# Scores of linear attention in 32x64 tiles of TensorE, without the quarter above the diagonal

## The reference

```python
qp = _phi(proj(Wq, bq)); kp = _phi(proj(Wk, bk)); v = proj(Wv, bv)      # _phi = elu + 1
def step(carry, inp):
    kv, ksum = carry
    kt, vt, qt = inp
    kv = kv + einsum('bhd,bhe->bhde', kt, vt)
    ksum = ksum + kt
    num = einsum('bhd,bhde->bhe', qt, kv)
    den = einsum('bhd,bhd->bh', qt, ksum)[..., None] + EPS
    return ((kv, ksum), num / den)
x = x + _linear_attn(_layernorm(x), ...) @ Wo.T + bo
x = x + ffn(_layernorm(x), gate_w, w1, b1, w2, b2)
```

## Time and profile before

| | us |
|---|---|
| median of 3 runs | 1938.83 (1938.12 to 1944.05) |
| the profiled execution | 1939.27 |
| its span in the profile | 1937.6 |
| PE, DVE, POOL, ACT busy | 1904.0, 1586.2, 891.4, 664.3 |
| mean granted clock of TensorE | 0.997 |

### The profile page before, as it was taken

One profiled execution on the slowest core, in us unless ns is written; L12 is line 12 of the kernel. 1 busy time (PEld: TensorE's weight loads), 2 busy tenths in 40 slices (PEclk: granted clock), 3 DMA queues, 4 the chain that ended last, 5 costly groups with the idle time before them and its releaser, 6 DMA issues. The chain is left out here.

```text
span 1937.6 us, 60626 instructions
## 1 busy us (share of the span) xinstructions
PE 1904.0 (98%) x25412; PEld 1671.4 (86%) x25412; DVE 1586.2 (82%) x3379; ACT 664.3 (34%) x1297; POOL 891.4 (46%) x979
## 2 busy tenths in 40 slices
PE   7999999999999999999999999999999999999997
PEld 6788888888888888888888888888888888888886
DVE  6878878887879888778878987887788897878787
ACT  4333333333333233333333333333332333323331
POOL 4355443455443554534554445545345544355422
PEclk9999999999999999999999999999999999999998
DMA  6343234433343432333423334323433334333222
GB/s 202 94 133 106 92 111 125 127 110 104 100 127 110 128 118 74 127 121 115 122 99 105 116 111 138 113 85 111 132 116 116 98 96 129 113 126 119 75 72 84
DMA packets 171202, 218.03 MB, mean 113 GB/s; under 512 B 24369, under 2 KB 85809, under 8 KB 170929
## 3 DMA queue, kind: packets, MB, share of 16 engines
q1 hardware_dynamic: 168528, 213.59, 34.7%
q10 hardware_dynamic: 2400, 0.55, 0.1%
HBM read 151.02 MB, written 63.04 MB: 110 GB/s over the span
## 5 line engine op out<-in xcount | busy, mean ns | idle before, releaser
L1258 POOL TENSOR_TENSOR k_sum<-k_sum,q_raw 128x512 f32<-128x512 f32 x128 | 165.0, 1290 | 556.2 <-DVE q_raw L933 556.2
L836 ACT ACTIVATE e_tmp<-ring,bias_n 128x512 f32<-128x512 f32 x256 | 176.1, 688 | 509.9 <-PE ring L651 506.8
L922 DVE TENSOR_TENSOR s_mask<-ring,causal 128x512 f32<-128x512 f32 x512 | 314.9, 678 | 0.0
L669 PE MATMUL ring<-wv_hi,xt_hi 128*128 128x260 f32 x1024 | 299.3, 292 | 0.0
L669 PE MATMUL ring<-wo_hi,o_hi 128*128 128x260 f32 x1024 | 287.8, 282 | 1.2 <-ACT o_hi L886 1.0
L669 PE MATMUL ring<-wv_lo,xt_hi 128*128 128x260 f32 x1024 | 288.8, 282 | 0.0
L669 PE MATMUL ring<-wv_hi,xt_lo 128*128 128x260 f32 x1024 | 288.8, 282 | 0.0
L669 PE MATMUL ring<-wo_lo,o_hi 128*128 128x260 f32 x1024 | 288.4, 282 | 0.0
L669 PE MATMUL ring<-wo_hi,o_lo 128*128 128x260 f32 x1024 | 287.3, 284 | 0.9 <-DVE o_lo L1170 0.9
L886 ACT ACTIVATE o_hi<-num_ps 128x512 fp32r<-128x512 f32 x128 | 76.4, 597 | 475.0 <-PE num_ps L750 474.9
L651 PE MATMUL ring<-xt_hi,wk_hi 128*128 128x512 f32 x512 | 207.9, 406 | 5.2 <-DVE xt_lo L998 3.2
(11 more groups left out here) (140 smaller groups left out, 4060.3 us busy)
## 6 DMA issues: line engine op xcount, KB each, us to landing
x_tok<-in_x SPq DMA_DIRECT2D x128, 256.0 KB, 3.7
res<-in_x SPq DMA_DIRECT2D x128, 256.0 KB, 2.8
out<-res SPq DMA_DIRECT2D x128, 256.0 KB, 2.1
x_in<-in_x_t SPq DMA_DIRECT2D x124, 256.0 KB, 4.6
keys_turned<-k_turned SPq DMA_DIRECT2D x112, 256.0 KB, 2.0
k_tok<-keys_turned SPq DMA_DIRECT2D x448, 64.0 KB, 2.0
x_rows<-moments_rows SPq DMA_DIRECT2D x31, 512.0 KB, 3.7
k_t<-in_wk_t SPq DMA_DIRECT2D x4, 256.0 KB, 8.3
```

Source lines behind the costliest of these rows:

```text
L669: mm = pe.matmul(bank[:, 0:HW], rows[a](k), w[b][:, k, h, :], start=n == 0, stop=n == 3 * KD - 1)
L836: act.activation(e_tmp[:, m], bank, ACT.Relu, bias=bias_n[:, m, g:g + 1], scale=-1.0).then_inc(phi_relu.handle, 1)
L922: dve.tensor_tensor(s_mask[:, j], ring[:, st.bank(u)].rearrange("p (g t) -> p g t", g=KD), repeat(causal, KD), ALU.mult).then_inc(free[st. ...
L1258: pool.tensor_tensor(k_sum[:, g], k_sum[:, g], q_raw[:, g], ALU.mult).then_inc(prod.handle, 1)
```

## The change

The scores of a tile are made in tiles of 32 rows and 64 columns, eight places of the array instead of four. Keys of the first 64 tokens (`lo`) are multiplied with all 128 queries, keys of the last 64 (`hi`) with the last 64 queries only; `hi` keys with the first 64 queries lie above the diagonal and are left out, their part of `s_mask` is set to zero once. For groups 0 and 1 the `lo` keys go to PSUM partitions 0 to 63 and the `hi` keys to 64 to 127; for groups 2 and 3 it is the other way round, so that two products of the same head stand in different halves of the array. The tokens of a tile then stand in swapped order for groups 2 and 3, in the scores, and so must they in the keys and values that these are multiplied with. The keys are swapped in the VectorE transpose, now two operations. The values are swapped through memory: a store of half a tile's values (128 KB) and two loads of 64 KB per tile, on SyncE's queue. The masks are six operations instead of four. The constants for the masks, the zeroes of `s_mask` and `order` are written by GpSimd after its first `rstds` (`set_masks`).

```diff
+HP = P // 2
...
+    values_dram = nc.dram_tensor("values_swapped", (TPB, P, DH), F32, kind="Internal").ap()
...
-    causal = sb("causal", [P, P])
+    causal_early = sb("causal_early", [P, HP])
+    causal_late = sb("causal_late", [P, KD, HP])
...
-    COLS, ROWS, BIASES, CONSTS = 4 * 16, 2 * 16, 3, 19 + E
+    COLS, ROWS, BIASES, CONSTS = 4 * 16, 2 * 16, 3, 26 + E
...
 
-    def set_constants(pool):
-        n = [2]
+    def linked_constants(pool, begun):
+        n = [begun]
 
...
             pool.wait_ge(const_set.handle, n[0])
-
+        return n, link
+    def set_constants(pool):
+        n, link = linked_constants(pool, 2)
         link(pool.memset(ones, 1.0))
-
-        link(pool.memset(causal, 1.0))
-        link(pool.affine_select(out=causal, in_=causal, compare_op=ALU.is_ge, fill=0.0, base=0,
-                                pattern=[[1, P]], channel_multiplier=-1))
 
...
                                     base=-g * HD, pattern=[[-1, 2 * 2 * HPG]], channel_multiplier=1))
+        assert n[0] == CONSTS - E - 9
+    def set_masks(pool):
+        n, link = linked_constants(pool, CONSTS - E - 9)
+        def keep_from(mask, base, pattern, fill=0.0):
+            link(pool.affine_select(out=mask, in_=mask, compare_op=ALU.is_ge, fill=fill, base=base,
+                                    pattern=pattern, channel_multiplier=-1))
+        link(pool.memset(s_mask, 0.0))
+        link(pool.memset(causal_early, 1.0))
+        keep_from(causal_early, 0, [[1, HP]])
+        keep_from(causal_early, HP - 1, [[0, HP]], fill=1.0)
+        keep_from(causal_early, HP, [[1, HP]])
+        link(pool.memset(causal_late, 1.0))
+        keep_from(causal_late[:, 0:2], HP, [[0, 2], [1, HP]])
+        keep_from(causal_late[:, 2:4], 0, [[0, 2], [1, HP]])
+        keep_from(causal_late[:, 2:4], HP - 1, [[0, 2], [0, HP]], fill=1.0)
         for e in range(E):
...
+    values_out, values_in = sem("values_out"), [sem(f"values_in{c}") for c in range(TPB)]
...
-            sp.wait_ge(keys_turned.handle, n + 1)
+            sp.wait_ge(keys_turned.handle, 2 * (n + 1))
...
 
+        def send_values(st, c):
+            b, u = st.off + 1, ("V", (c, 1))
+            sp.wait_ge(free[BANK[u]].handle, st.freed(u))
+            if b:
+                sp.wait_ge(values_in[c].handle, 32 * b)
+            sp.dma_start(values_dram[c], v_tok[:, c, DH:]).then_inc(values_out.handle, 16)
+        def fetch_values(st, c):
+            b = st.off + 1
+            sp.wait_ge(values_out.handle, 16 * (TPB * b + c + 1))
+            for h in range(2):
+                to, of = slice(h * HP, (h + 1) * HP), slice((1 - h) * HP, (2 - h) * HP)
+                sp.dma_start(v_tok[to, c, DH:], values_dram[c, of]).then_inc(values_in[c].handle, 16)
         def load_res(st, off, c):
...
                 load_res(st, t + 1, 0)
-                send_keys(t + 1, 0)
-                fetch_keys(t + 1, 0)
+                for c in range(TPB):
+                    if c == TPB - 1:
+                        send_keys(t + 1, 0)
+                        fetch_keys(t + 1, 0)
+                    send_values(st, c)
+                    fetch_values(st, c)
                 return
...
                 if c == 2:
+                    if st.has("proj"):
+                        send_values(st, 0)
                     send_keys(t, 3)
+                    if st.has("proj"):
+                        fetch_values(st, 0)
                     fetch_keys(t, 3)
+                    if st.has("proj"):
+                        send_values(st, 1)
                 if last and st.has("proj"):
+                    send_values(st, 2)
                     send_keys(t + 1, 0)
+                    fetch_values(st, 2)
                     fetch_keys(t + 1, 0)
...
                     spread_moments(st)
+                if last and st.has("proj"):
+                    send_values(st, 3)
                 if st.has("proj") or last:
                     store(st, c)
+                if st.has("proj") and c >= 2:
+                    fetch_values(st, 1 if c == 2 else 3)
 
...
                 pe.wait_ge(free[st.bank(u)].handle, st.claimed(u))
-            for g in range(KD):
+            lo, hi = slice(c * P, c * P + HP), slice(c * P + HP, (c + 1) * P)
+            def product(j, u, g, keys, queries, rows_out):
+                rows, first = slice(j * HD, (j + 1) * HD), queries.start - c * P
+                out = ring[rows_out:rows_out + HP, st.bank(u), g * P + first:(g + 1) * P]
+                return pe.matmul(out, k_t[rows, par, g, keys], q_div[rows, par, g, queries],
+                                 start=True, stop=True, skip_group_check=True, tile_position=(j * HD, rows_out))
+            for g in range(KD // 2):
+                other = g + KD // 2
                 if c == 0:
-                    pe.wait_ge(free[BANK[("R", g)]].handle, st.freed(("R", g)))
+                    for r in (g, other):
+                        pe.wait_ge(free[BANK[("R", r)]].handle, st.freed(("R", r)))
                 for j, u in enumerate(scores_of(c)):
-                    rows = slice(j * HD, (j + 1) * HD)
-                    mm = pe.matmul(ring[:, st.bank(u), g * P:(g + 1) * P], k_t[rows, par, g, t], q_div[rows, par, g, t],
-                                   start=True, stop=True, skip_group_check=True, tile_position=(j * HD, 0))
-                    if g == KD - 1:
+                    product(j, u, g, lo, t, 0)
+                for j, u in enumerate(scores_of(c)):
+                    product(j, u, other, lo, t, HP)
+                for j, u in enumerate(scores_of(c)):
+                    product(j, u, g, hi, hi, HP)
+                for j, u in enumerate(scores_of(c)):
+                    mm = product(j, u, other, hi, hi, 0)
+                    if g == KD // 2 - 1:
                         mm.then_inc(full[st.bank(u)].handle, 1)
...
+            pe.wait_ge(values_in[c].handle, 32 * (st.off + 1))
...
         def mask_scores(st, c):
-            for j, u in enumerate(scores_of(c)):
+            banks = [st.bank(u) for u in scores_of(c)]
+            assert banks == list(range(banks[0], banks[0] + HPG))
+            for u in scores_of(c):
                 dve.wait_ge(full[st.bank(u)].handle, st.filled(u))
-                dve.tensor_tensor(s_mask[:, j], ring[:, st.bank(u)].rearrange("p (g t) -> p g t", g=KD),
-                                  repeat(causal, KD), ALU.mult).then_inc(free[st.bank(u)].handle, 1)
+            scored = ring[:, banks[0]:banks[0] + HPG].rearrange("p j (g t) -> p j g t", g=KD)
+            for rows, gs in ((slice(0, HP), slice(0, KD // 2)), (slice(HP, P), slice(KD // 2, KD))):
+                early = causal_early[rows].unsqueeze(1).unsqueeze(1).to_broadcast([HP, HPG, KD // 2, HP])
+                dve.tensor_tensor(s_mask[rows, :, gs, 0:HP], scored[rows, :, gs, 0:HP], early, ALU.mult)
+            for j, k in enumerate(banks):
+                dve.tensor_tensor(s_mask[:, j, :, HP:P], scored[:, j, :, HP:P], causal_late, ALU.mult
+                                  ).then_inc(free[k].handle, 1)
 
...
                 dve.wait_ge(keys_out.handle, 16 * n)
-            dve.transpose(k_turned.rearrange("p j (g b) -> p g j b", g=KD),
-                          k_t[:, b % 2, :, c * P:(c + 1) * P].rearrange("p g (j a) -> p g j a", j=HPG)
-                          ).then_inc(keys_turned.handle, 1)
+            out = k_turned.rearrange("p (s j) (g b) -> p g s j b", s=2, g=KD)
+            keys = k_t[:, b % 2, :, c * P:(c + 1) * P].rearrange("p g (s j a) -> p g s j a", s=2, j=HPG // 2)
+            for gs, order in ((slice(0, KD // 2), 1), (slice(KD // 2, KD), -1)):
+                dve.transpose(out[:, gs], keys[:, gs, ::order]).then_inc(keys_turned.handle, 1)
 
...
-        run(pool, body)
+        run(pool, body, lambda: set_masks(pool))
```

## The result

The changed kernel takes 1978.41 us (median of four runs, 1972.21 to 1982.29), where the kernel before, on the same chips, took 1941.25 (1938.12 to 1944.05). The ratio is 1.0189, 95% interval [1.0155, 1.0222]: 1.9% slower, where 1% faster was forecast, and 44 us above the top of the range. The profiled execution took 1979.34 us, its span 1977.6, at a mean granted clock of 0.994. The span grew by 40.0 us.

A forecast was written before the change was run, and what follows sets the result against it. TensorE was taken to set the time in every block. From 1939.3 us, 28.2 came off for the scores and 4.0, 2.9 and 0.6 were added for waits: 1918.6 us, range 1905 to 1934.

The forecast's parts named there:

- The stage of scores: TensorE's score products per tile: 0.88 us instead of 1.10, ends 0.84 and 0.91, saving 28.2 us over 128 stages.
- The first fill: Start of a scores' stage: a place's second row begins 0.16 us after its first, with weights of 64 columns.
- the step of 128 columns: Scores on TensorE: 0.11 us from one 128-column row of a place to its next, for eight places as for four.
- that of 64: Scores on TensorE: a step of 64 columns takes 0.057 us, bounds 0.03 and 0.11.
- VectorE's masks and the third tile's output product: Six mask operations take 2.52 us against 2.40; the output product waits 0.13 us in 31 blocks, 4.0 us lost.
- "No wait" for the fourth tile: Fourth tile's output product: first bank free at 1006.50, TensorE comes at 1006.76, so no wait for the masks.
- The first rival: VectorE becomes the bound at the third tile and next block's keys: about 1943 us, down to 1934; chance 0.12.
- Transfers: SyncE's queue: one store and two loads of values per tile, 384 issues, cost nothing; 5 us of cover for keys.
- the fourth rival: Value transfers delay keys or residual loads beyond 5 us, each us more costing 31 us: 1950 or so; chance 0.04.
- The third rival: The two fours of places take turns in written order: stage 1.24 us, +18 us, 1957 us; chance 0.07.
- Constants: GpSimd's mask constants, behind its first moments, take at most 10.4 us together and cost nothing; VectorE asks at 20.48.
- The signs named for failure: Prediction wrong if the scores' stage is near 1.1 us or longer, or TensorE's waits for VectorE exceed 15 us.

The follow-up runs named there:

- g_no_state: The changed kernel without the product of the state with the queries, 32 rows fewer per tile ahead of the scores: 1927.74 us, ratio 0.9942 to the kernel before.
- i_both: The changed kernel without the exchange of values through memory and with four masks of 128x512 elements as before: 1956.32 us, ratio 1.0099 to the kernel before.
- a_no_values: The changed kernel without each tile's store and two loads of values and TensorE's wait for them: 1965.94 us, ratio 1.0131 to the kernel before.

## Why the prediction was wrong, step by step

**The stage of scores: the step that failed.** Forecast 0.88 us, measured 1.03, saving 9 us and not 28.2. The first fill, the step of 128 columns, that of 64 and the eight places side by side were right for the first 32 rows: cut off at chosen instants, the changed kernel's stage reads

```profile
1039.80 0.65 PE L773 MATMUL ring<-q_div,k_t 32*64 32x128 f32 x33
...
1039.80 0.81 PE L773 MATMUL ring<-q_div,k_t 32*64 32x128 f32 x37
...
1039.80 0.88 PE L773 MATMUL ring<-q_div,k_t 32*64 32x128 f32 x41
...
1039.80 0.95 PE L773 MATMUL ring<-q_div,k_t 32*64 32x128 f32 x47
...
1039.80 1.05 PE L773 MATMUL ring<-q_div,k_t 32*64 32x128 f32 x61
...
1040.83 0.50 PE L702 MATMUL ring<-xt_hi,wk_hi 128*128 128x512 f32 x1
```

for cuts at 0.39, 0.50, 0.60, 0.70 and 0.84 us after its start, and the projection behind. 33 rows have started by 0.39, as forecast (0, 0.16, 0.27, 0.33, 0.385 for eight each). The next four need 0.11 us, the four after them 0.10, where forecast rows would come eight within 0.05. From the records, row 33 starts at 0.383, row 34 at 0.462, and the last of 64 at 0.885 instead of 0.66 + 0.05: 16 ns a row on average, rows 34 to 49 mostly one every 16 to 17 ns, with one step of 0.06 us. The old kernel's update of the state changes its rhythm at the same row when it is given 64 rows, though there the form of the products changes too; the stages of 32 rows have no such place. With 32 rows fewer ahead of the scores (`g_no_state`) the break stands at the same row. It is not the order in the code (the exchange left the end of the stage where it was). That columns play no part isn't shown: behind row 32, rows of 128 columns came some 17 ns apart, rows of 64 some 11 and rows of one, with narrower weights, 9.5. What the runs fit, and no run shows by itself, is that 32 rows with their 32 weight loads stand ready when a stage may begin, and that the rest arrives at a pace of its own. The Trainium skill (TensorE: Matmul & The Clock Gate, Part 1, Architectural detail) says that TensorE's queue is 64 instructions deep. By that page the break would come behind 32 weight loads and 32 matmuls, and the trace agrees, 33 rows by 0.39 us. The prediction took four and eight places' steps from stages of 32 rows and applied them to one of 64; every row that it rested on was one of the first 32 of its stage. That is why the bounds agreed and all were too short.

**Standstills in the scores: not in the prediction at all.** They cost 18.4 us in the scores, and of the 8.0 us in the K projections 1.3 by a standstill there and 2.8 through the clock. The timeline of the longest:

```profile
373.99 1.07 PE L773 MATMUL ring<-q_div,k_t 32*64 32x128 f32 x53
378.00 0.36 PE L773 MATMUL ring<-q_div,k_t 32*64 32x64 f32 x11 [2.94 <-issue]
378.29 0.50 PE L702 MATMUL ring<-xt_hi,wk_hi 128*128 128x512 f32 x1
```

TensorE stops after 53 of 64 rows of one stage, where it has no wait left to pass. The DMA queues from 375.2 to 376.6 (packets, MB, share of sixteen engines' time):

```profile
q1 hardware_dynamic: 329, 0.34, 100.3%
q8 instruction: 1, 0.02, 6.0%
```

One packet of the program is fetched in this window; by its record it took 1.35 us from 375.24, and the rows resume 1.41 us after its end. I compared each standstill over 0.2 us behind the start-up with the record of the packet before it. In the changed kernel there are ten in the scores and five in the projections behind them, two of these at the first row: all fifteen end 1.05 to 1.54 us after the end of such a packet. In the other kernels of this shape, and in the old shape with more rows, they too lie between 1.0 and 1.7. The nine that the profile puts down to the masks show no such bond (1.9 to 4.8 us). A packet comes once in 8.4 us, so fifteen standstills that all end within the same half microsecond behind one are not chance. So the cause is the supply of instructions. The change brought 8192 more instructions of TensorE (4096 rows and their weight loads) and 32 more packets, so a packet holds 256: two stages of scores. The speed of a stage alone doesn't make it late, as `g_no_state` has the same stage of 128 instructions in 1.03 us; it is late in stretches of 320 instructions. Removing 32 rows from the stretch all but removed the standstills (two runs, with rests of other kinds in both), adding 32 to the old kernel brought them, less traffic shortened them. When a fetch is asked for, and how much stands ready at that moment, no run showed.

**The clock.** The windows of the changed kernel around that standstill (window, length, busy of PE, PEld, DVE, ACT and POOL with instructions, granted clock, DMA share, GB/s):

```profile
374.00:376.00 2.00, 1.06 (x57) 0.93 (x54) 1.51 (x3) 0.91 (x3) 1.23 (x1) 1.00 1.12 252
376.00:378.30 2.30, 0.30 (x12) 0.23 (x11) 0.00 (x0) 0.92 (x3) 0.03 (x1) 1.00 1.03 333
378.30:382.40 4.10, 4.10 (x17) 3.23 (x13) 3.74 (x8) 0.00 (x0) 0.00 (x0) 0.67 0.31 112
```

After 2.9 us of rest, and 1.7 us after the rows resume, the granted clock is 0.5, so 1.2 GHz instead of 2.4, for 3.4 us, and the K projection takes 4.14 instead of the 2.85 us usual behind the scores. There are four such stretches before the last block, at 38, 69, 380 and 1103 us, where the kernel before has none up to 1923. Their K projections are 1.2 to 1.6 us longer than the same ones before, 5.6 of the 8.0 us. Only the last two, 2.8 us, follow a standstill without a releaser (2.9 and 2.1 us); the one at 69 follows a wait of 3.1 us for `xt_lo`, and the one at 38 comes in the kernel with the transfers alone too. The standstill of 2.4 us at 743 had none behind it: the length of the rest alone doesn't decide.

**VectorE's masks and the third tile's output product.** The step was right in kind and too small. Its neighbours' overlap did not carry over to the half-height operations:

```profile
1015.56 1.33 DVE L993 TENSOR_TENSOR s_mask<-ring,causal_early 64x512 f32<-64x512 f32 x2
1016.90 1.41 DVE L995 TENSOR_TENSOR s_mask<-ring,causal_late 128x256 f32<-128x256 f32 x4
1018.24 1.04 DVE L1259 SCALAR_TENSOR_TENSOR rden<-rden_high,lo_rows,den 128x256 fp32r<-128x256 f32 x1
...
1025.47 1.28 DVE L1072 TENSOR_TENSOR xt_lo<-x_in,xt_hi 128x512 fp32r<-128x512 f32 x2
```

Two early ones take 1.34 us and not 1.20, all six 2.68 and not 2.52 (2.40 before). The first bank comes free 1.34 + 0.41 us after the start of the masks, so the wait is near 0.27 by the prediction's own sum; measured, the V projection with the wait behind it went from 2.97 to 3.21 us, +0.24 per block where 0.13 was forecast; with four longer cases, this tile lost 8.9 us in 31 blocks. "No wait" for the fourth tile was wrong: the masks come late there when what precedes them does.

```profile
543.41 2.67 DVE L1072 TENSOR_TENSOR xt_lo<-x_in,xt_hi 128x512 fp32r<-128x512 f32 x2
...
547.27 1.37 DVE L993 TENSOR_TENSOR s_mask<-ring,causal_early 64x512 f32<-64x512 f32 x2
548.66 1.42 DVE L995 TENSOR_TENSOR s_mask<-ring,causal_late 128x256 f32<-128x256 f32 x4
```

Two `xt_lo` that take 1.28 us in an ordinary block (above) take 2.67, the first late bank is free at 549.07, and the output product waits 1.17 us, to 549.23. What holds these two up is GpSimd, which neither the prediction nor a rival has:

```profile
542.30 1.56 POOL L1327 TENSOR_TENSOR x_in<-x_in,x_rows 128x512 f32<-128x512 f32 x1
543.79 1.75 POOL L1403 TENSOR_TENSOR res<-res,bo_row 128x512 f32<-128x512 f32 x1
```

The first `xt_lo` ends 0.55 us after the first of these, the second 0.55 us after the second. Of the changed kernel's 124 `xt_lo` of this line, all 17 that began with over 0.25 us of a GpSimd operation still to run took 0.88 to 2.07 us instead of 0.68, and in the kernel before all ten such took 0.85 to 1.77. The masks and `o_lo`, which read PSUM, never took over 0.70. The forecast weighed one ordinary block and gave this place 0.26 us to spare. The median block has no wait here indeed (2.99 us from values to output product, 2.98 before), but behind the first block nine of 31 went over 3.2 us, and this tile lost 9.0 us in them all. 7.7 of these lie in six blocks, each with an `xt_lo` of over 1.7 us beside GpSimd; the kernel before has one such block, with 0.3 us lost. Four masks instead of six took away 13.0 us where the prediction has 4.0 + 2.9 for all waits on VectorE. The first rival had the mechanism and, at the third tile, the price (0.30 us in 31 blocks, 9.3 against 8.9); the 15.5 us that it put at the next block's keys didn't come (one wait of 3.1 us for `xt_lo`), and it missed the fourth tile.

**Transfers.** "Cost nothing" was wrong. Alone 3.8 us, in the changed kernel 12.5. The cover on SyncE's queue was counted and held in all blocks but the last: there TensorE waits 2.6 us for keys, as it does in the kernel with the transfers alone (3.1), and not at all in the kernel before and in `i_both`, and 0.3 us in `a_no_values`. This is the fourth rival's mechanism in one place. What wasn't counted is that other transfers and operations take longer beside them: `x_tok` landed after 4.4 us instead of 3.7, and GpSimd stood 46.1 us waiting for the rows of moments instead of 25.2, so GpSimd's work comes later and meets `xt_lo`, up to the masks behind it; without the exchange two blocks had an `xt_lo` of over 1.7 us in tile 3, and not six:

```profile
L1325 POOL TENSOR_TENSOR x_in<-x_in,x_rows 128x512 f32<-128x512 f32 x124 | 200.3, 1615 | 46.1 <-DMA x_rows<-moments_rows 46.1
...
x_tok<-in_x SPq DMA_DIRECT2D x128, 256.0 KB, 4.4
```

That this chain is the whole of the 12.5 us was argued from these rows; the runs show only the total, the wait for keys, and that less traffic shortens standstills.

**The rest.** The third rival, written order, was excluded by the runs: its stage would be 1.24 us. Its time, 1957, is that of the kernel with both side effects undone, by chance. Constants did cost something. VectorE never waited for them, as forecast, but GpSimd's first memset runs beside the normalisation of the first tokens, which took 3.37 us instead of 1.92 (before, then after; in the kernel with the transfers alone, which has no such memset, it took no longer than before):

```profile
10.29 1.92 DVE L986 TENSOR_SCALAR x_tok<-x_tok,mv 128x512 f32<-128x512 f32 x4 [1.59 <-POOL mv L1243]
...
10.30 3.37 DVE L1060 TENSOR_SCALAR x_tok<-x_tok,mv 128x512 f32<-128x512 f32 x4 [1.59 <-POOL mv L1317]
...
10.22 1.81 POOL L435 MEMSET s_mask<- 128x2048 f32 x1
```

The first projection begins 1.5 us later for it, and most of that is gone again by the second K projection. The signs named for failure came: a stage of 1.03, nearer to 1.1 than to the forecast's 0.91, and over 15 us of waits for VectorE (9.2 + 3.4 + 3.1 = 15.7 against 8.6 in the earlier trace rows). An engine waiting for its own program, and VectorE held up by GpSimd, were on no list.

## What to carry to other kernels

Count instructions, not only columns: here a split of small float32 products into twice as many rows kept the engine 7% shorter in the stage and then cost twice the gain in standstills, since 160 rows in a stretch outran their supply at times where 128 hardly did. A duration taken from a stage of 32 rows says nothing about the 33rd. And where a change both shortens TensorE's stage and lengthens the VectorE work that hands banks back, compare the two over all blocks, late ones included, not in one typical tile; what GpSimd does beside VectorE belongs into that comparison.

## What the hardware showed that was not expected

- Behind 32 rows of small float32 products (64 instructions with the weight loads), further rows of a scores' stage started 16 ns apart on average, to 0.885 us, where the first 32 had started within 0.37 us.
- TensorE stood still up to 2.9 us with no semaphore to wait for, ending 1.05 to 1.7 us after a 16 KB packet on the instruction queue.
- After rests of 2.1 and 2.9 us the granted clock was 0.5 for 3.4 us, which made the K projections there 1.5 and 1.3 us longer; after one of 2.4 us it stayed at 1.
- A passage from small products to large ones, or back, cost about 0.1 us each.
- A VectorE product of 64x512 elements out of PSUM took 0.67 us, as long as one of 128x512 (0.68 in the earlier trace rows): half the partitions saved nothing.
- A VectorE subtraction (`xt_lo`, 0.68 us) or normalisation (`x_tok`, 0.53 us) between on-chip buffers, begun while a GpSimd operation ran, ended about 0.55 us after that operation (up to 2.07 us for one `xt_lo`) or 0.3 us after it (`x_tok`, 2.0 us); the operations that read PSUM weren't lengthened.
